# Audio tower kernel: queries and keys from one product, scores computed at the end of the preceding unit

## What is computed

```
h = nx @ expand                      # 128 -> 16 + 16 + 256 + 256
q, k = h[..., :16], h[..., 16:32]
gated = linear * gelu(pre_gelu, exact)
local, v = gated[..., :128], gated[..., 128:]
mask = where(causal, sigmoid(rel + position_bias_mult), -inf)
logits = einsum('bqd,bkd->bqk', q, k) / sqrt(16) + mask
attn = einsum('bqk,bkd->bqd', softmax(logits), v)
return x + concatenate([local, attn]) @ project
```

## Time and profile before

| | us |
|---|---|
| median of 3 runs | 804.38 |
| lowest, highest | 804.24, 805.21 |
| the profiled execution | 804.39 |
| its span, first to last instruction | 802.70 |
| PE busy | 778.9 (97% of the span) |
| DVE busy | 674.7 (84%) |
| ACT busy | 504.3 (63%) |
| POOL busy | 288.6 (36%) |
| sum of the residual of unit 0, 1, 2, 3 at | 547.02, 579.04, 613.57, 647.80 |
| of unit 4, 5, 6, 7 at | 680.88, 713.96, 747.05, 777.71 |

### The profile page before, as it was taken

How to read it: one execution, slowest core, us unless ns; L and a number is a source line. 1 busy time by engine, 2 the same in 40 slices (tenths; PEclk the granted TensorE clock), 3 DMA queues, 4 the chain that set the end, 5 groups by cost and what they waited for, 6 DMA issues and landing times. The chain is left out here.

```text
span 802.7 us, 15609 instructions
## 1 busy us (share of the span) xinstructions
PE 778.9 (97%) x5555; PEld 475.5 (59%) x5555; DVE 674.7 (84%) x1608; ACT 504.3 (63%) x1100; POOL 288.6 (36%) x291
## 2 busy tenths in 40 slices
PE   9899999999999999999999999999999999999997
PEld 5354564564564564564563343367878788787785
DVE  3797998999899899899899889648788887787956
ACT  3275776776777677677677677655554636546333
POOL 4355241241342342342644245312436342333222
PEclk9799999999999999999999999999999999999999
DMA  4509143143143145135125300010000000000001
GB/s 112 78 18 122 11 61 85 15 62 84 15 63 83 15 57 88 15 53 92 16 44 81 67 7 5 9 14 8 2 21 1 20 20 2 21 1 20 20 2 38
DMA packets 85676, 31.08 MB, mean 39 GB/s; under 512 B 58496, under 2 KB 84320, under 8 KB 85600
## 3 DMA queue, kind: packets, MB, share of 16 engines
q1 hardware_dynamic: 85024, 29.61, 22.4%
q10 hardware_dynamic: 576, 0.49, 0.4%
HBM read 4.76 MB, written 3.06 MB: 10 GB/s over the span
## 5 line engine op out<-in xcount | busy, mean ns | idle before, releaser
L464 ACT ACTIVATE probs<-ps_a 128x384 f32<-128x384 f32 (+1 forms) x732 | 301.0, 480 | 129.1 <-PE ps_a L668 126.7
L552 DVE TENSOR_REDUCE neg_max<-ps_a 128x1 f32<-128x512 f32 (+1 forms) x384 | 247.9, 677 | 39.6 <-PE ps_a L684 36.1
L668 PE MATMUL ps_a<-q_rep,k_rep 98*128 98x384 bf16 (+3 forms) x768 | 231.8, 324 | 1.7 <-DMA q_rep<-max_T 1.0
L684 PE MATMUL ps_a<-k_rep,q_rep 96*128 96x512 bf16 (+3 forms) x768 | 218.3, 327 | 8.0 <-DVE neg_max L552 4.9
L699 PE MATMUL ps_pv<-probs,v_hat 128*32 128x364 f32 (+3 forms) x1536 | 135.6, 482 | 1.2 <-DVE out_r L531 0.6
L668 PEld LDWEIGHTS ps_a<-q_rep,k_rep 98*128 98x128 bf16 (+1 forms) x768 | 77.3, 102 | 94.9 <-issue 37.7
L684 PEld LDWEIGHTS ps_a<-k_rep,q_rep 96*128 96x128 bf16 (+1 forms) x768 | 75.1, 103 | 86.9 <-DVE neg_max L552 27.0
L554 DVE TENSOR_REDUCE neg_max<-ps_a 128x2 f32<-128x472 f32 x192 | 122.7, 639 | 0.0
L699 PEld LDWEIGHTS ps_pv<-probs,v_hat 128*32 128x32 f32 (+1 forms) x1536 | 42.7, 109 | 60.9 <-issue 40.5
L2009 POOL TENSOR_TENSOR out_n<-out_r,inv_sum 128x192 f32<-128x192 f32 x32 | 16.3, 511 | 157.4 <-DVE inv_sum L533 149.2
L279 POOL TENSOR_SCALAR qk_e<-qk_e 128x748 f32<-128x748 f32 x14 | 38.0, 2714 | 25.7 <-ACT qk_e L370 25.7
(11 more groups left out here) (239 smaller groups left out, 1182.3 us busy)
## 6 DMA issues: line engine op xcount, KB each, us to landing
k_rep<-parts_k SPq DMA_DIRECT2D x96, 96.0 KB, 3.8
q_rep<-parts_q SPq DMA_DIRECT2D x93, 96.0 KB, 4.0
hall<-out_n SPq DMA_DIRECT2D x256, 12.0 KB, 1.8
xT<-in_x SPq DMA_DIRECT2D x8, 375.0 KB, 3.7
out_h<-y_out SPq DMA_DIRECT2D x7, 320.0 KB
q_rep<-max_T SPq DMA_DIRECT2D x32, 6.0 KB
w_sb<-in_w_T SPq DMA_DIRECT2D x2, 256.0 KB, 3.5
out_h<-y_out SPq DMA_DIRECT2D x8, 54.0 KB
```

The source lines that it names most:

```text
L464: act.activation(probs[0:rows(kt), n % RING, 0:w], ps_a[0:rows(kt), 3 + n % 3, 0:w], ACT.Exp, scale=DH ** -0.5).then_inc(p_ready, 1)
L552: dve.tensor_reduce(neg_max[0:rows(t), 0, col:col + 1], ps_a[0:rows(t), c, :], AX.X, ALU.max, negate=True).then_inc(sc_max, 1)
L668: pe.matmul(out[0:rows(kt), 0:QW[qh]], k_rep[0:KM, cb % 2, h, kt * P:kt * P + rows(kt)], q_rep[0:KM, cb % 2, qh, h, 0:QW[qh]], start=True, ...
L684: last = pe.matmul(out, q_rep[0:KS, it % 2, t // QT, h, t % QT * P:t % QT * P + rows(t)], k_rep[0:KS, it % 2, h, 512:L] if c == 2 else k_r ...
```

## The change

Five things are changed.

1. One product gives queries and keys: `qk_w3` holds the query weights three times and the key weights three times, 96 columns in all. The three rows of parts of each are made once (`high`, `left`, `middle`, `rest` without a j), with `take_3` in the place of `take_out`. The parts stand in `part_a`, and SP's new `spread_qk` copies them with five DMAs into `qk_rep`, which now has two buffers.
2. `scores` of unit it+1 stand at the end of iteration it on PE: three behind `turn_att`, three behind `project`. `row_max` of the first three stands before `sum_2` on DVE, `row_max` of the last three and `maxima` behind `statistics_3`. Unit 1 keeps its scores in its own iteration.
3. `turn_max` stands behind the values and the second local product, `turned_max` on ACT behind the gelu of the latter.
4. `qk` stands between the second and third `ffn1`; `high` and `middle` on ACT stand among `hidden` and the exponentials, `left` on DVE behind `choose`, and `rest` between the first and second weighing (`weigh`). In iteration 0 `qk` stands in the middle of `attend`.
5. DVE's turning of the last outputs stands at the head of the second part. DVE repeats the weights twice more in the first part, POOL makes 8 more constants.

The planner's order (`order_of`) follows, so the banks change. The core of the diff:

```diff
-    qk_rep = sb("qk_rep", [KM, 2, LP], BF16)
+    qk_rep = sb("qk_rep", [KM, 2, 2, LP], BF16)
+    qk_w3 = sb("qk_w3", [P, 2, 3, QK], F32)
+    take_3 = sb("take_3", [KS, 2], F32)
...
-        if t == 0:
-            pe.wait_ge(S["x_rep"], n * 2 + 2)
+        if t == 0 and n == 0:
+            pe.wait_ge(S["x_rep"], 2)
+        elif t == 0:
+            pe.wait_ge(S["x_spread"], 80 * n)
...
+        def spread_qk(n):
+            def move(j, at, src):
+                sp.dma_start(qk_rep[at:at + src.shape[0], n % 2, j, 0:L], src).then_inc(S["x_spread"], 16)
+
+            if n > 1:
+                sp.wait_ge(S["y_st"], (n - 1) * NT)
+            sp.wait_ge(S["x_part_a"], n)
+            move(0, 0, part_a[0:3 * QK, 0, :])
+            move(1, 5 * QK, part_a[5 * QK:6 * QK, 0, :])
+            sp.wait_ge(S["x_last"], n)
+            move(0, 3 * QK, part_a[0:3 * QK, 1, :])
+            move(1, 0, part_a[3 * QK:6 * QK, 1, :])
+            move(1, 3 * QK, part_a[3 * QK:5 * QK, 1, :])
...
+        def left(n):
+            dve.wait_ge(S["x_part_a"], n)
+            dve.scalar_tensor_tensor(in_two(left_a[:, 0, :]), in_two(part_a[:, 0, :]), take_3[:, 0:1], halves("qk", n)[0:KS],
                                      ALU.mult, ALU.add).then_inc(S["x_left"], 1)
...
+        def rest(n):
+            dve.wait_ge(S["x_part_b"], n)
+            dve.scalar_tensor_tensor(part_a[:, 1, :], part_b[:, 0, :], take_3[:, 1:2], left_a[:, 0, :],
+                                     ALU.mult, ALU.add).then_inc(S["x_last"], 1)
...
+        turn_outputs(dve, ps_pv, B - 1, 3)
         dve.memset(table[:, :], 0.0).then_inc(setup, 1)
...
-        def qk(n, j):
-            o = take("qk", n, j, "x_left", n * 2 + j - 1)
-            if j == 0:
-                pe.wait_ge(S["x_nx2T"], n + 1)
+        def qk(n):
+            o = take("qk", n, 0, "x_left", n)
+            pe.wait_ge(S["x_nx2T"], n + 1)
             for h in range(2):
-                last = pe.matmul(o[0:KS, 512 * h:512 * h + HALF], qk_w[:, j, :, :].rearrange("p a c -> p (a c)"),
+                last = pe.matmul(o[0:KS, 512 * h:512 * h + HALF], qk_w3[:, :, :, :].rearrange("p j a c -> p (j a c)"),
```

More of the change, by code:

```diff
@@ L1481, in _ @@
         turned_2(1)
-        for j in range(2):
-            high(1, j)
+        high(1)
+        middle(1)
         turned_att(0)
-        for j in range(2):
-            middle(1, j)
         for it in range(1, B + 1):
@@ L1512, in _ @@
                     exponential(it, k)
[L1513 to L1515 removed]
+                    if x and k == 0:
+                        middle(it + 1)
             if z:
@@ L1696, in _ @@
                 statistics_3(it - 1)
+            if it > 1 and y:
+                for t in range(3, NT):
+                    G["row_max"](dve, flat("scores", it, t), it, t)
+                G["maxima"](dve, it)
             if it == 0:
@@ L1703, in _ @@
                     local(it, j)
+                left(it + 1)
+                rest(it + 1)
+                attended(it)
                 G["normalise"](dve, it + 2)
-                attended(it)
-                for j in range(2):
-                    left(it + 1, j)
-                for j in range(2):
-                    rest(it + 1, j)
                 sum_2(it)
@@ L1753, in _ @@
                 transform(it - 1, 1)
-            if x:
-                rest(it + 1, 0)
-                rest(it + 1, 1)
             if z and it < B:
                 gates(it - 1)
+            if x:
+                for t in range(3):
+                    G["row_max"](dve, flat("scores", it + 1, t), it + 1, t)
             if y:
@@ L1845, in attend @@
             for t in range(NT):
+                if between and t == 3:
+                    between()
                 pe.wait_ge(S["y_p"], n * NT + t + 1)
@@ L1924, in _ @@
         turn_2(1)
-        attend(0)
-        for j in range(2):
-            qk(1, j)
+        attend(0, lambda: qk(1))
         turn_att(0)
@@ L1935, in _ @@
                 values(it, 1)
+            if it == 1:
                 for t in range(3):
                     scores(it, t)
+            if y:
                 local(it, 1)
+            if it == 1:
+                for t in range(3, NT):
+                    scores(it, t)
+            elif y:
+                turn_max(it)
             if w:
@@ L1944, in _ @@
                 turn_2(it + 1)
-            if y:
-                for t in range(3, NT):
-                    scores(it, t)
             if z:
@@ L1980, in _ @@
                 turn_att(it)
+            if x:
+                for t in range(3):
+                    scores(it + 1, t)
+            if y:
                 project(it)
+            if x:
+                for t in range(3, NT):
+                    scores(it + 1, t)
 def build(nc, x, wq, wk, wv, bq, bk, bv, expand, project, pos_mult, router_T, w1_T, b1, w2_T, b2, out):
```

168 lines of the change are left out of this document (87 added, 81 removed).

## The result

The changed kernel takes 828.74 us (median; 827.71 to 831.01), the kernel before 804.31 in the same comparison: a ratio of 1.031, 95% interval 1.028 to 1.033. The prediction was 824.0, with a range of 813 to 845. The profiled execution took 827.71 us, of which the span is 826.0, 23.3 more than before; the prediction's terms add up to 19.5.

What follows compares the result with a forecast made beforehand. PE was taken to bound the gated units; removed products and new waits summed as 0.3 + 4.05 + 2.65 + 3 x 3.15 + 2.9 + 0.2 = 19.5 us more than 804.38, giving 824.0, range 813 to 845.

Steps and rivals of the forecast that it cites:

- (a): Head of unit 4: PE waits 0.31 us before the first local product, for banks that the residual sum reads.
- (b): Before the values, unit 4: PE waits 2.11 us (0.7 to 3.6) for score banks DVE frees after sum and statistics.
- (d): Before the logits, unit 4: PE waits 0.49 us for ACT's copy of nx3T, which scores no longer cover.
- (e): Attended product, unit 4: waits of 0.3 before the first weighed piece and 1.4 before the next, together 1.73 us.
- The step of 1.5 through POOL's residual: Unit 2: DVE's last statistics operation, slow beside POOL's residual, delays the maxima and lengthens the wait before the values by 1.5 us.
- The attended output: Unit 2: the last batch's statistics delay the attended output, for which PE has no spare time; 0.8 us (0 to 1.24).
- the fall of the clock: Rival: gaps at unit starts, likeliest unit 2, drop PE's clock; 4.6 us each, one 828.6; several units 833 to 852, chance 0.27.
- Unit 3: Unit 3: 2.65 us more than before, including 0.65 for half of unit 2's delay.
- The first part: Before the gated units: 0.2 us more (0 to 0.5) for DVE's extra weight repeats.
- Units 0 and 1: Units 0 and 1 with the border of the two parts: 0.3 us more, between -2 and +3.
- The smaller wait: Rival: the wait for banks before the values stays, but none at the attended product; 815 us, chance 0.12.
- The faster one: Rival: DVE frees the score banks before PE asks, leaving only removed products and border; 794.5 us, chance 0.07.

Runs made afterwards that it cites:

- the first experiment: The changed kernel with DVE reducing the last three scores and splitting the maxima in front of the statistics; 816.15 us, ratio to the kernel before 1.015.
- the last: One product, moved border and copies first in SP's queue, with POOL's residual of units 3 and 4 moved behind the inverse root; 794.43 us, ratio 0.987.

## Why the prediction was right, and where it was short

**What bounds.** Right. PE's busy row was the right one to go by: taking one product of 1.28 us away alone shortened the steady unit by 1.4. The Trainium skill ("Trainium Kernel Development and Optimization", Performance Expectations) calls matmul busy time a bad metric for the distance to roofline and the weight loads' the good one. The prediction asked whether the removed product might then buy nothing; it bought 1.4 us a unit, and the measurement decides.

**(a), (b), (d).** Right to 0.02 us each, from starts and durations of rows of before. That (b) is DVE's order, not the banks as such, is shown by the first experiment. The low end given for (b), 0.7 with the maxima in front of the statistics, was too high: in that experiment PE does not wait there at all.

**(e).** The size was near: 0.4 to 0.6 before the first piece and 1.26 less its 0.23 before the second, together 1.5 to 1.6, against 1.73. The cause was only half right. "The copy `middle` between two exponentials on ACT is over before DVE asks" holds as it is worded: it ends at 682.32, and DVE takes up `rest` at 682.50 without a wait. What the prediction left out is that `middle` pushes the second exponential back, and with it a bank of the attended product and the second piece. Moving `rest` alone brought the second piece forward by 0.46, and DVE then waited for ACT.

**Unit 2.** The step of 1.5 through POOL's residual was right in mechanism and size: 3.38 of wait, and 1.5 less with the residual moved. The attended output cost 0.4 to 0.6, not 0.8. (The terms given for this unit add up to 38.5, not 38.6.) What the sum left out is the fall of the clock, which the prediction had as a rival with unit 2 as its likeliest place, at 4.6 us a fall. It came there, and cost 1.7: the price was taken from the long stretch at the beginning of the execution, while this fall lasted some 3.5 us. It is nearly the whole miss of 1.5 in this unit. That the rival's figure for one fall, 828.6, is almost the measured median is luck: the profiled execution has two falls of 1.7, not one of 4.6.

**Unit 3** was 0.3 over, since a POOL operation one step earlier also lies on DVE's short one (0.9, not the 0.65 assumed).

**The first part.** 0.2 was predicted, 1.59 measured, and one fall of the clock around 430 costs 1.7, in a stretch that the change leaves alone. The eleven kernels of the experiments have the first part of the changed kernel, one of them but for the border; it ended between 524.17 and 527.53 in them. Six of the eleven have this fall, as the changed kernel has, and five have not. In four of these five the stretch at the lower clock early on the earlier trace rows also cost 1.7 less; the fifth differs from the kernel before in neither fall, and its first part ended at 525.77, against 525.90. So the fall belongs to the single execution, and a cost of the change here is not shown.

**Units 0 and 1** came to 0.62 with the border against 0.3. The median lies another 1.0 above the profiled execution. Two of its four executions, 829.6 and 831.0, have a mean granted clock of 0.986; the other two, 827.7 and 827.9, have 0.990. More of the same falls would explain it, but no trace of these executions shows it.

**The rivals.** The smaller wait (815) failed, both waits are there together. The faster one was right about its point: with the reductions earlier, the wait goes. But nx3 and the attended pieces keep it from 794.5. What reached that time, by another way, was one product with the moved border and the copies first.

## What to carry to other kernels

Before work is moved across engines, ask for every buffer that the next product takes whose reader frees it, and what stands in front of that reader in its own list; starts and durations of the old trace gave three of four waits here to some hundredths of a microsecond. The fourth was 0.1 to 0.2 off and its cause half wrong, because an operation had also been put in front of a reader on a second engine, ACT. Test the parts of a change apart: here two of five, the product and the border, were together worth 1.1% once the copies stood first in their queue, and all five cost 3%. What the border adds to that was not run apart. The DMAs added to SP's queue waited once for what stood ahead in it, at the one place where it was full; look there first when only one unit is slow.

## What the runs showed of the hardware

A short DVE operation on six columns took 1.68 us in place of 0.17 beside a POOL operation, ended with it, and was back at 0.17 once that stood elsewhere. Twice the slowness then went to another short operation (1.73 in the first experiment, 1.76 in the last). `kept` took 1.81 beside POOL's 1.47, and 0.56 in unit 2 of the changed kernel. The last three row maxima, which read PSUM, took 2.26 beside POOL's 1.33 in the changed kernel and beside its 1.81 in the first experiment alike; the first three took 1.07 with POOL idle (unit 4 of the changed kernel) and 1.08 beside it (unit 1). By the Trainium skill ("SBUF — State Buffer", Who interferes with whom) DVE and POOL share a port pair that one of them holds for a whole instruction, and a reduction does not take part; the trace agrees with both.

The granted clock fell to the 1.2 GHz level behind idle times of PE of 3.4, 2.7, 2.1 and 1.9 us, and stayed at 2.4 GHz behind others of 2.8 and 1.9. The same code did both: behind the border's idle 1.50 us the clock held in the kernel before and fell in the one with the product alone, and behind the 1.13 us of the first part it held before and fell in the changed kernel. By the Trainium skill ("TensorE: Matmul & The Clock Gate", HAM oscillation) idle gaps between bursts bring it down; that agrees, but which of several like gaps is hit differed, and what decides it stays open. In unit 2 it fell in all four kernels whose profile has 2.1 us or more of idle time before the values, and in none of the other four kernels of the changed order, where it is 1.9 us or less. With `rest` and `middle` last, five units in a row (2 to 6) had it. Most falls at PE's waits cost 1.7 us, so a wait of about 2 us can cost nearly twice its length. Two lasted twice as long, 7 us: unit 1 of the kernel with the product and the border, and unit 2 with `rest` and `middle` last.
